# Pacing the last row gathers by their own landings and no longer by TensorE's progress

## The chip, the cores and the metric

The kernel runs on one core of a Trainium2 chip, and the time is the device time of one execution in microseconds (us). The kernel before takes 754.92 us, the median of three runs that lie between 752.6 and 755.72 us.

## The reference

The kernel computes one transformer block over 2048 tokens of 512 numbers: a cross-attention, and then a feed-forward part in which each token goes through two of eight experts and through one shared expert, which is kept here as two halves. Only the end of it matters for the change:

```python
wmat = (jax.nn.one_hot(topk_i, N_EXPERTS) * topk_w[..., None]).sum(axis=1)
e = jnp.einsum('ntf,nhf->nth', jax.nn.silu(g) * u, down_w)
routed = jnp.einsum('nth,tn->th', e, wmat)
shared = jax.nn.silu(sg) * su @ sh_down_w.T
return (routed + shared).reshape(B, S, H)
```

So every row of the output is the residual, plus the shared expert's result, plus two rows of expert results with two weights.

## The kernel before

Tokens are handled in 16 tiles of 128. The feed-forward part is a row of 68 units, numbered by `w`. A unit is one gate-and-up product (`gate_up`, 24 matmuls of 128x352, lines 1521 to 1525), a nonlinear step on ScalarE and VectorE, and one down product (`down`, 9 matmuls of 128x512, line 1538). Units 0 to 15 are the shared expert's two halves over the first eight tiles, units 16 to 51 are 36 slots of routed tokens (their results go to `slot_y` in DRAM), and units 52 to 67 are the shared halves over the last eight tiles. `C0` is 52, the number of the first late unit; `EARLY` is 8.

TensorE's order in the late units is: gate-and-up of `w`, down of `w-2`, gate-and-up of `w+1`, down of `w-1`, and so on. Between the two products of a unit lie, in this order: ScalarE's SiLU (line 1142), VectorE's product (line 2040), ScalarE's square (line 1147), VectorE's scale (2045), and the two fp16 parts of the hidden tile (ScalarE 1152, VectorE 2053). Then SyncE issues a DMA transpose of that tile into `hT` (`h_rows`, line 644). TensorE's down product waits for its landing (`hT_ld`), and so does the SiLU of the unit two later, because it overwrites the same hidden tile. Two `hT` tiles are used in turn.

GpSimd issues the gathers. For each of the 16 token tiles (numbered by `q`) two indirect DMAs of 128 rows of 2 KB, 256 KB together, read the tile's two expert results from `slot_y` (line 952) into `gather_1[q]` and `gather_2[q]`, each tile with buffers of its own. Ahead of the first one GpSimd waits until the last slot result has landed in DRAM (`y_st`). A semaphore `gat_ld[q % 4]` counts 32 for each tile. VectorE combines the gathered rows with the residual and the shared result in its late units (`early_out` for the first eight tiles, lines 2451 and 2455; `late_out` and `late_gathered` for the others, lines 2477, 2482, 2491, 2495), and each of these waits for `gat_ld`. GpSimd has nothing to do after the gathers.

All other late transfers are on SyncE's queue, in program order: in two units one activation tile (`load_late`), two residual tiles (`load_res`), two output tiles (`store_out`), 256 KB each, and the two transposes. `u_ready` counts the units whose up product is done on TensorE.

Of the kernel before, what the change touches and what calls it, by code (L numbers as in the profile page):

```python
# [84 lines left out]
def build(nc, x, ctxT, wqT, wkvT, wfcT, bfc, gwT, wgu, wdn, out):  # L85
# [17 lines left out]
    with ExitStack() as ctx:  # L103
# [3 lines left out]
        def sem(name):  # L107
            return ctx.enter_context(nc.semaphore(name))
# [287 lines left out]
        g_ready, u_ready, sil_done = sem("g_ready"), sem("u_ready"), sem("sil_done")  # L396
# [11 lines left out]
        B0, C0 = PA, PA + PB  # L408
# [375 lines left out]
        def _(pool):  # L784
# [160 lines left out]
                pool.wait_ge(y_st[s], FREE + 16 * ((SLOTS + 1 - s) // 2))  # L945
            for q in range(2 * EARLY):
                t = q // 2 + q % 2 * EARLY
                pool.wait_ge(u_ready, C0 + 3 + 2 * q // 3)
                if q >= 4:
                    pool.wait_ge(gat_ld[q % 4], q // 4 * 32)  # L950
                for to, idx in ((gather_1[q], p1_i), (gather_2[q], p2_i)):
                    nc.gpsimd.indirect_dma_start(  # L952
                        out=to, out_offset=None, in_=slot_y,
                        in_offset=bass.IndirectOffsetOnAxis(ap=idx[:, t:t + 1], axis=0)).then_inc(gat_ld[q % 4], 16)
# [1670 lines left out]
```

## Time and profile before

| | us |
|---|---|
| median of three runs | 754.92 |
| lowest, highest | 752.6, 755.72 |
| the profiled execution's own time | 754.92 |
| its span, first to last instruction | 753.1 |
| TensorE busy in the span | 732.2 |
| VectorE busy | 561.1 |
| ScalarE busy | 419.0 |
| GpSimd busy | 272.1 |
| mean share of the DMA engines, bytes per time | 223 GB/s over the span |

The span is what the profiler saw between the first and the last instruction; 1.8 us of the execution lie outside it. TensorE ran at its full granted clock of 2.4 GHz in all of it (mean 0.998 of full speed). A busy time is the time an engine was working, whatever waited for it; to find what sets the end, one has to ask which engine has no idle time in a stretch, and that is what the rows below are for.

### The profile page before, as it was taken

The numbers are of one execution on the slowest core, as the hardware profiler recorded it, in microseconds if no ns is written. First come the engines' busy times: TensorE is split into PE (matmuls) and PEld (weight loads), VectorE is DVE, ScalarE is ACT, GpSimd is POOL, SyncE is SP. The second block draws the span as 40 slices with busy tenths as digits, with TensorE's granted clock in tenths as the row PEclk, the third lists the DMA queues.
The fourth block names the chain that finished last, engine by engine and source line by source line (L and its number), as shares of the span: only waits on it lengthen the run. The fifth ranks groups of instructions, "written<-read, shape, count | busy, mean of one in ns | idle before, by whom it ended". The sixth has DMA issues, their size and how long they took to land.

```text
span 753.1 us, 16125 instructions
## 1 busy us (share of the span) xinstructions
PE 732.2 (97%) x5325; PEld 398.9 (53%) x5326; DVE 561.1 (75%) x1191; ACT 419.0 (56%) x845; POOL 272.1 (36%) x221
## 2 busy tenths in 40 slices
PE   6998999999999999999999999999999999999998
PEld 3554533434444334656665566555555556655554
DVE  4777689999999967788589998655555555546776
ACT  3667468888888884777543454343433334223222
POOL 3264006999997311664400401212111121016540
PEclk9999999999999999999999999999999999999999
DMA  9898946755755798997578664977767779549993
GB/s 328 332 409 282 252 147 187 221 168 176 220 150 151 249 344 301 345 386 281 190 204 259 153 155 123 197 175 181 184 168 184 173 180 213 127 124 283 329 308 92
DMA packets 155100, 168.17 MB, mean 223 GB/s; under 512 B 97952, under 2 KB 111776, under 8 KB 154528
## 3 DMA queue, kind: packets, MB, share of 16 engines
q1 hardware_dynamic: 143724, 126.20, 57.6%
q0 software_dynamic: 10720, 40.12, 17.0%
q10 hardware_dynamic: 596, 1.07, 0.4%
q8 instruction: 36, 0.59, 0.4%
q14 instruction: 24, 0.20, 0.1%
HBM read 104.09 MB, written 41.42 MB: 193 GB/s over the span
## 4 chain that ended last, share of the span: by engine, by line
PE 53%; DVE 23%; DMA 8%; issue 6%; POOL 4%; ACT 3%; SPq 2%; DVEq 0%; POOLq 0%; ACTq 0%
PE psum L1521 21%; DVE sb_rows L1786 12%; PE psum L1538 11%; PE psum L1523 4%; PE psum L1448 4%; PE psum L1257 4%; POOL sb_weights L952 4%; DMA sb_weights<-k_parts 2%; DMA sb_weights<-in_wdn 2%; PE psum L1540 2%; PE psum L1233 1%; DVE sb_rows L1915 1%; PE psum L1281 1%; DMA x_dram<-sb_rows 1%; DMA sb_rows<-xb_dram 1%
## 5 line engine op out<-in xcount | busy, mean ns | idle before, releaser
L1521 PE MATMUL psum<-sb_weights,sb_rows 128*128 128x352 f16 (+1 forms) x1344 | 209.7, 313 | 0.0
L1521 PEld LDWEIGHTS psum<-sb_weights,sb_rows 128*128 128x128 f16 x1344 | 131.2, 98 | 76.1 <-issue 1.2
L1786 DVE TENSOR_REDUCE sb_rows<-psum 128x4 f32<-128x1024 f32 x128 | 150.0, 1214 | 4.6 <-PE psum L1281 4.5
L1073 ACT ACTIVATE sb_weights<-psum 128x512 f32<-128x512 f32 x256 | 139.4, 595 | 22.8 <-PE psum L1353 19.7
L1538 PE MATMUL psum<-sb_weights,sb_hT 128*128 128x512 f16 (+1 forms) x522 | 122.2, 379 | 0.0
L1147 ACT ACTIVATE psum<-psum 128x352 f32<-128x352 f32 x68 | 30.5, 448 | 124.9 <-DVE psum L2040 112.3
L933 POOL DMA_INDIRECT sb_rows<-xn_rows,sb_slot_tok x36 | 34.6, 960 | 176.7 <-DVE sb_rows L2418 134.8
L1353 PE MATMUL psum<-sb_weights 50*128 50x512 f16 x256 | 86.6, 387 | 1.7 <-ACT sb_weights L1073 0.9
L1367 PE MATMUL psum<-sb_weights 128*32 128x256 f32 x1024 | 82.6, 394 | 0.3
L1538 PEld LDWEIGHTS psum<-sb_weights,sb_hT 128*128 128x128 f16 x522 | 50.9, 98 | 54.0 <-issue 0.6
L1281 PE MATMUL psum<-sb_weights 48*128 48x256 f16 x512 | 70.7, 274 | 1.6 <-DMA sb_weights<-k_parts 0.9
L1448 PE MATMUL psum<-sb_weights 128*128 128x512 f32 x128 | 58.3, 598 | 0.5 <-ACT sb_weights L1079 0.4
L2053 DVE SCALAR_TENSOR_TENSOR sb_h<-psum,sb_h_scale_i,sb_h 128x352 f16<-128x352 f32 x68 | 39.7, 583 | 22.7 <-ACT sb_h L1152 19.5
L952 POOL DMA_INDIRECT sb_weights<-slot_y,sb_p_i x32 | 32.5, 1015 | 64.4 <-DMA slot_y<-sb_rows 41.9
L2040 DVE SCALAR_TENSOR_TENSOR psum<-psum,sb_inv_now,sb_h 128x352 f32<-128x352 f32 x36 | 21.3, 592 | 43.6 <-issue 31.0
L1353 PEld LDWEIGHTS psum<-sb_weights 50*128 50x128 f16 x256 | 23.4, 93 | 54.2 <-ACT sb_weights L1073 44.7
L1142 ACT ACTIVATE sb_h<-psum,sb_inv_now 128x352 f32<-128x352 f32 x36 | 20.0, 555 | 49.4 <-PE psum L1521 37.7
L1257 PE MATMUL psum<-sb_weights 128*128 128x512 f16 x192 | 44.9, 380 | 2.3 <-DVE sb_weights L1852 1.2
L1152 ACT ACTIVATE sb_h<-psum,sb_h_scale_i 128x352 f16<-128x352 f32 x68 | 37.7, 555 | 16.2 <-DVE sb_h_scale_i L2045 14.8
L838 POOL TENSOR_TENSOR sb_weights<-sb_weights,sb_w_scale_i 128x1408 f32<-128x1408 f32 x15 | 38.0, 2533 | 23.6 <-ACT sb_weights L1119 22.8
L848 POOL TENSOR_TENSOR sb_weights<-sb_weights 128x1408 f16<-128x1408 f32 x15 | 43.0, 2864 | 1.2
L1142 ACT ACTIVATE sb_h<-psum,sb_w_inv_i 128x352 f32<-128x352 f32 x32 | 17.8, 556 | 33.1 <-PE psum L1521 22.7
(307 smaller groups left out, 1172.8 us busy)
## 6 DMA issues: line engine op xcount, KB each, us to landing
sb_weights<-in_wgu SPq DMA_DIRECT2D x20, 704.0 KB, 7.1
sb_weights<-in_wgu POOLq DMA_DIRECT2D x20, 704.0 KB, 6.8
sb_weights<-in_wdn SPq DMA_DIRECT2D x17, 768.0 KB, 6.3
slot_y<-sb_rows SPq DMA_DIRECT2D x36, 256.0 KB, 2.4
sb_weights<-q_parts SPq DMA_DIRECT2D x96, 64.0 KB, 3.0
x_dram<-sb_rows SPq DMA_DIRECT2D x24, 256.0 KB, 4.6
q_parts<-sb_weights SPq DMA_DIRECT2D x16, 256.0 KB, 4.1
sb_rows<-in_x POOLq DMA_DIRECT2D x16, 256.0 KB, 5.8
```

Source lines behind the costliest of these rows:

```text
L848: nc.gpsimd.tensor_tensor(low, stage, high, ALU.subtract).then_inc(gu_cut, 1)
L952: nc.gpsimd.indirect_dma_start(out=to, out_offset=None, in_=slot_y, in_offset=bass.IndirectOffsetOnAxis(ap=idx[:, t:t + 1], axis=0)).then_ ...
L1073: nc.scalar.activation(probs[G % 2][:, kt, pair * 512:(pair + 1) * 512], bank[4 + f % 2], ACT.Exp, scale=exp_by[n]).then_inc(exp_done, 1)
L1257: mm = nc.tensor.matmul(bank[Q_BANKS[n][m]], wq16[:, wp, k, m * P:(m + 1) * P], xnT[n % 2][:, xp, k, :], start=(k == 0 and i == 0), stop=( ...
L1281: mm = nc.tensor.matmul(bank[banks[qt] + side][:, h * SEQ:(h + 1) * SEQ], q_st[s][lo:hi, g, h, b * SEQ + qt * P:b * SEQ + (qt + 1) * P], k ...
L1353: nc.tensor.matmul(bank[4 + side].rearrange("p (h t) -> p h t", h=HH), k_st[s][lo:hi, g, b * SEQ + kt * P:b * SEQ + (kt + 1) * P], q_st[s] ...
L1367: mm = nc.tensor.matmul(bank[6][VW * c:VW * (c + 1), 0:SEQ], v_now, probs[G % 2][:, kt, c * SEQ:(c + 1) * SEQ], start=(kt == 0), stop=(kt ...
L1448: mm = nc.tensor.matmul(bank[2 + s][:], oT[s][:, k, :], wfc_sb[:, k, :], start=(k == 0), stop=(k == KD - 1))
L1521: mm = nc.tensor.matmul(to[:, 0:F], x_T[:, at:at + P], gu(wp, k, which), start=first, stop=last)
L1538: mm = nc.tensor.matmul(bank[Y_BANKS[par]][:], hT[par][:, hp, j, :], dn(wp, j), start=first, stop=last)
L1786: nc.vector.tensor_reduce(to[:, :, j // UB, :, j % UB, qt], psum[:, banks[qt] * 512:(banks[qt] + 2) * 512] .rearrange("p (a h k) -> p a h ...
L2053: nc.vector.scalar_tensor_tensor(h16[par][:, 1, 0:F], bank[GU_BANKS[par][1]][:, 0:F], h_scale[:, par:par + 1], h16[par][:, 0, 0:F], ALU.mu ...
```

## The change

The list of waits ahead of each tile's two gathers is made anew. Before, every tile waited until TensorE's up product of a unit fixed by `q` was done, and from `q` = 4 on also until the gathers of tile `q-4` had landed. After, tiles 1 to 3 wait for an up product, and tiles 4 to 15 only for the landing of tile `q-4`; tile 0 has no wait of its own.

```diff
@@ -945,9 +945,10 @@
                 pool.wait_ge(y_st[s], FREE + 16 * ((SLOTS + 1 - s) // 2))
             for q in range(2 * EARLY):
                 t = q // 2 + q % 2 * EARLY
-                pool.wait_ge(u_ready, C0 + 3 + 2 * q // 3)
                 if q >= 4:
                     pool.wait_ge(gat_ld[q % 4], q // 4 * 32)
+                elif q > 0:
+                    pool.wait_ge(u_ready, C0 + 2 + q)
                 for to, idx in ((gather_1[q], p1_i), (gather_2[q], p2_i)):
                     nc.gpsimd.indirect_dma_start(
                         out=to, out_offset=None, in_=slot_y,
```

The number that `u_ready` had to reach was 55, 55, 56, 57 for tiles 0 to 3, then 57, 58, 59, 59, 60, 61, 61, 62, 63, 63, 64, 65. It is now 55, 56, 57 for tiles 1 to 3 and nothing for the others.

## Rows read from the trace of the kernel before

**Rows 1.** The page: busy time of each engine; granted clock in 40 slices.
```profile
PE 732.2 (97%) x5325; PEld 398.9 (53%) x5326; DVE 561.1 (75%) x1191; ACT 419.0 (56%) x845; POOL 272.1 (36%) x221
PEclk9999999999999999999999999999999999999999
```
**Rows 2.** Timeline of TensorE, from 715 us; a bracket would show idle time.
```profile
720.92 2.11 PE L1538 MATMUL psum<-sb_weights,sb_hT 128*128 128x512 f16 x9
...
726.45 2.11 PE L1538 MATMUL psum<-sb_weights,sb_hT 128*128 128x512 f16 x9
...
744.96 1.24 PE L1711 MATMUL psum<-sb_weights,sb_hT 128*128 128x512 f16 x5
746.74 0.51 PE L1703 MATMUL psum<-sb_tri,sb_h 128*128 128x128 f16 x6 [0.54 <-DVE sb_h L2053]
```
**Rows 3.** Timeline of GpSimd, the gathers: start, duration, idle before.
```profile
674.07 0.94 POOL L952 DMA_INDIRECT sb_weights<-slot_y,sb_p_i  x1 [41.86 <-DMA slot_y<-sb_rows]
675.32 0.95 POOL L952 DMA_INDIRECT sb_weights<-slot_y,sb_p_i  x1 [0.30 <-issue]
...
683.15 0.95 POOL L952 DMA_INDIRECT sb_weights<-slot_y,sb_p_i  x1 [1.36 <-PE psum L1521]
...
685.66 0.95 POOL L952 DMA_INDIRECT sb_weights<-slot_y,sb_p_i  x1 [0.30 <-issue]
...
689.36 0.95 POOL L952 DMA_INDIRECT sb_weights<-slot_y,sb_p_i  x1 [0.98 <-PE psum L1521]
...
728.13 0.94 POOL L952 DMA_INDIRECT sb_weights<-slot_y,sb_p_i  x1 [0.30 <-issue]
```
**Rows 4.** Line 952: what ended GpSimd's idle time before a gather (us, times).
```profile
  DMA slot_y<-sb_rows: 41.9, 1
  PE psum L1521: 15.8, 9
```
**Rows 5.** Chain of waits from 716 to 727 us: start, length, what.
```profile
719.60 5.33 DMA sb_weights<-slot_y,sb_p_i
724.93 0.03 issue
724.96 0.76 DVE sb_weights L2477
```
**Rows 6.** Timeline of VectorE: first use of gathers; the operation ahead of 724.96 us.
```profile
679.44 0.74 DVE L2451 SCALAR_TENSOR_TENSOR sb_zero_row<-sb_weights,sb_w,sb_zero_row 128x512 f32<-128x512 f32 x1
...
724.46 0.58 DVE L2053 SCALAR_TENSOR_TENSOR sb_h<-psum,sb_h_scale_i,sb_h 128x352 f16<-128x352 f32 x1 [0.42 <-ACT sb_h L1152]
```
**Rows 7.** Timeline of SyncE's queue: two issues of the transpose of the hidden tile.
```profile
719.55 1.21 SPq L644 DMA_TRANSPOSE sb_hT<-sb_h  x1
...
741.62 1.21 SPq L644 DMA_TRANSPOSE sb_hT<-sb_h  x1
```
**Rows 8.** Timeline of ScalarE: the SiLU that a transpose released.
```profile
726.00 0.56 ACT L1142 ACTIVATE sb_h<-psum,sb_w_inv_i 128x352 f32<-128x352 f32 x1 [1.58 <-DMA sb_hT<-sb_h]
```
**Rows 9.** DMA from 686 to 730 us: busy tenths in 40 slices; packets; two queues.
```profile
DMA  9999999989999989999899999999999999999989
...
DMA packets 11928, 14.49 MB, mean 329 GB/s; under 512 B 7184, under 2 KB 7184, under 8 KB 11927
...
q1 hardware_dynamic: 9985, 8.10, 66.7%
q0 software_dynamic: 1942, 6.38, 41.5%
```
**Rows 10.** Windows: busy us by engine, granted clock, DMA share, GB/s.
```profile
685.00:690.00 5.00, 5.00 (x31) 2.89 (x30) 3.56 (x7) 1.29 (x3) 3.41 (x4) 1.00 1.23 360
...
707.00:718.00 11.00, 11.00 (x68) 6.41 (x66) 8.62 (x17) 3.10 (x8) 5.92 (x6) 1.00 1.07 367
718.00:729.00 11.00, 11.00 (x68) 6.41 (x67) 7.75 (x18) 3.50 (x11) 5.65 (x7) 1.00 1.07 304
729.00:740.00 11.00, 11.00 (x67) 6.45 (x66) 8.69 (x17) 3.10 (x7) 0.08 (x1) 1.00 0.65 194
```

## The prediction

> **What bounds the kernel now.** I read the page first: TensorE is busy in 97% of the span and at its full granted clock in every slice [rows 1]. Then I read the timeline of each engine over the stretch in which the gathers run, because GpSimd's busy time on the page says nothing of who waits for it. On TensorE's timeline one unit's down product starts at 720.92 us and the next one's at 726.45, so a unit lasts 5.53 us, and the rows carry no bracket, which is to say no idle time. The first idle time on TensorE after the gathers start is 0.54 us at 746.74, and it waits there for VectorE, for the last hidden tile [rows 2]. So from 674 us to the end the span is a sum of TensorE's own matmuls, with 0.54 us beside them.
>
> The gathers are issued from 674.07 to 728.13 us [rows 3]. The last slot result's landing holds the first one (41.9 us of idle time, once), and TensorE's up products hold nine later ones, 15.8 us together [rows 4]. Does anyone wait for a gather? The chain of waits says so: a gather issued at 719.60 takes 5.33 us and releases VectorE at 724.93 [rows 5]. But VectorE was in its operation of 724.46, 0.58 us long, up to then, and started the next one at 724.96 with no bracket [rows 6]. The landing and the end of the operation fell together. Nobody lost time to it, and TensorE was busy beside it.
>
> **The change, part by part.** *Tiles 0 to 3.* Tile 0 loses a wait for 55 up products; the one that ended last there was the landing of the slot result, so it starts at 674.07 as before [rows 3, 4]. For tiles 1, 2 and 3 the old numbers were 55, 56, 57 and the new ones are C0 + 2 + q = 55, 56, 57: the same. Cost 0, and the first eight gathers stay where they are. One of the nine waits for TensorE, that at 683.15, is tile 3's and stays [rows 3].
>
> *Tiles 4 to 15.* The other waits go; what is left is the landing of the tile four back. GpSimd issues one gather each 1.25 us when nothing holds it (674.07, 675.32) [rows 3], so a tile each 2.5 us, and three tiles and one gather lie between a tile's second gather and the tile four on: 3 x 2.5 + 1.25 = 8.75 us. A gather landed after 5.33 us with the DMA busy [rows 5]; the first tile's second gather, issued at 675.32, was used at 679.44, so at most 4.1 us after [rows 3, 6]. Both are under 8.75, so the wait that is left will mostly be open, and the change does what it says: from 685.66 on, 24 gathers in a row, the last issued at 685.66 + 23 x 1.25 = 714.4 us where it was 728.13, or 13.7 us earlier. On GpSimd nothing is queued behind, and no instruction is added; the wait instructions removed are GpSimd's. Gain on the path: nothing, as long as VectorE finds its rows in time, which it did. What idle time could be given back on TensorE is the 0.54 us at 746.74, and that is no gather's. So the gain is between 0 and 0.5 us; I take 0.
>
> *What the gathers now collide with.* The price can only come through the DMA engines. SyncE's queue carries the transposes of the hidden tile, and TensorE's down product waits for each. The one issued at 719.55 landed at 726.00, when the SiLU that it held was released (6.45 us), and TensorE started that unit's down product at 726.45 [rows 2, 7, 8]. That was 0.45 us to spare. With no gather about, the one issued at 741.62 had landed by 744.96, when its down product starts without idle time: at most 3.34 us [rows 2, 7]. So gathers and bulk transfers can cost a transpose 3 us, and there is room for 6.45 + 0.45 = 6.9 us.
>
> How full are the DMA engines? From 686 to 730 us every one of 40 slices shows 8 tenths or more; SyncE's queue (q1) takes 66.7% and the gathers (q0) 41.5%, together 108% [rows 9]. A share over 100% means that packets overlap, so I size it twice. By shares: 6.38 MB in gathers of 0.262 MB are 24 gathers, and 41.5% of 44 us is 18.3 us, or 0.76 us each. After, 24 gathers fall in 30 us: 24 x 0.76 / 30 = 61%, and with q1's 66.7% the sum is 128%, where the most that five us show is 1.23 and eleven us 1.07 [rows 10]. By bytes: q1 moves 8.10 MB / 44 us = 184 GB/s, the gathers after 6.3 MB / 30 us = 210 GB/s, together 394, against 367 in the best window of 11 us [rows 9, 10]. That is short by 7%, which over 30 us is 2.2 us of DMA work that doesn't fit.
>
> Who pays these 2.2 us? The gathers have 8.75 - 5.33 = 3.4 us before their own wait closes, and nobody needs them early. SyncE's queue has about half a microsecond to spare in the tightest unit. Bounds: below, 0 (the gathers give way, or the transposes that fall into slack of several us absorb it); above, 6 us (the first rival). I take the middle of the bytes' sum: 1.1 us of idle time on TensorE, in one to three down products between 690 and 720 us. From about 716 us on the gathers are gone and q1 is nearly alone, as from 729 on now (share 0.65) [rows 10]; the transpose of 719.55 then lands sooner than 6.45 us, which gives nothing back, because TensorE was not waiting for it.
>
> **Sum.** The profiled execution took 754.92 us, which is also the median; its span is 753.1, and 1.8 us lie outside. 754.9 - 0 + 1.1 = 756.0 us. The likeliest case's own range is 754.0 to 758.5.
>
> **The rivals.** *First, slower: turn by turn.* If each DMA engine shares itself half and half between the two queues whenever both have work, SyncE's queue gets 50% where it needs 66.7%. The 24 gathers hold 18.3 us of DMA work, so both queues contend for 36.6 us; in that time SyncE's queue does 18.3 us of work and needs 0.667 x 36.6 = 24.4. It falls 6.1 us behind, a slip that TensorE must wait for: 754.9 + 6.1 = 761.0. It decides from the point where a transpose takes over 6.9 us unit after unit; then the SiLU two units later is held as well [rows 8] and the loop feeds itself. For it: the 6.45 us at 719.55. Against it: q1 took 66.7% beside 41.5%, so it was not held to half, and GpSimd's own wait closes at 8.75 us.
>
> The Trainium skill, "DMA: Bandwidth & Descriptors", section "Queues, rings and completion order", says that each DMA engine goes round among the queues that have work and changes over a packet at a time. That is a rule that speaks against this change; by it the time would be nearer 761 than 756. The trace before agrees only so far that transposes are late when gathers are about, and doesn't show the turns.
>
> *Second, no effect: the gathers are hidden either way.* The transfers of SyncE's queue keep their pace, the shortfall falls on the gathers alone, and TensorE has no new idle time: 754.9 us. For it: windows with 1.23 and 367 GB/s without a gap on TensorE [rows 10]. Against it: the 0.45 us to spare.
>
> *Third, faster: the chain is right.* If the landing at 724.93 did hold VectorE, an earlier gather would start the following operations sooner; the profile gives 0.03 us there [rows 5], and TensorE can give back no more than 0.54 us [rows 2]: 754.4 us, still no change to be measured.
>
> **Chances.** What a measurement of this kernel can tell from no change is about 0.5%, or 3.8 us: under 751.1 or over 758.7. The forecast, 0.2 to 3.8 us slower, holds 0.50. The second rival holds 0.18, the third 0.06; both are within 0.5%. The first, over 758.7, holds 0.23. To a gain of over 0.5%, for which I can name no term, I leave 0.03. So faster 0.03, same 0.74, slower 0.23. The range reaches from 753.2 (the second and third with the scatter of the runs) to 760.0, into the first rival.
>
> **What would show it.** In the changed profile the last gather is issued near 714 us and line 952's idle time that TensorE ends falls from nine times to one, from 15.8 us to 1.4. If gathers reach 8.75 us, GpSimd's idle time is released by a DMA instead: the shortfall landed on the gathers. TensorE's first down products after 690 us show brackets that add up to 1 us (forecast), 0 (second) or 6 (first), and ScalarE's line 1142 waits for the transpose more often than once. The share after 720 us falls toward 0.65. The prediction is wrong if brackets on TensorE exceed 3.8 us, if the first eight gathers move, or if VectorE shows a wait for a gather at all.

## The result, and the profile after

The changed kernel takes 779.57 us (median of four runs, 776.47 to 780.23) where the kernel before takes 754.53 us (four runs, 752.6 to 755.72). The ratio is 1.0318 with a 95% interval of 1.0291 to 1.0346: 25 us slower, and 19.6 us over the upper end of my range.

The profiled execution took 776.41 us, among the fastest of the changed kernel, and 21.5 us more than the profiled one before. What the profiles explain is these 21.5 us; the other 3.5 us between the medians are in no profile.

The page of the changed kernel, to compare with [rows 1]: the engines do the same work, and the granted clock falls in two of the last four slices.

```profile
PE 737.8 (95%) x5325; PEld 399.1 (52%) x5326; DVE 562.1 (73%) x1191; ACT 418.6 (54%) x845; POOL 271.2 (35%) x221
PEclk9999999999999999999999999999999999996799
```

GpSimd's timeline of the changed kernel, to compare with [rows 3]. It did what I had forecast: the first eight gathers stayed, and the other 24 followed, most of them 1.25 us apart (three take 1.3 to 1.5 us and not 0.95, so the mean is 1.30), the last at 714.95. One gather is 128 rows of 2 KB, so 256 KB; a tile's two are 512 KB together, and not 256 as the description of the kernel has it.

```profile
682.44 0.94 POOL L953 DMA_INDIRECT sb_weights<-slot_y,sb_p_i  x1 [2.10 <-PE psum L1522]
683.69 0.95 POOL L953 DMA_INDIRECT sb_weights<-slot_y,sb_p_i  x1 [0.30 <-issue]
...
714.95 0.95 POOL L953 DMA_INDIRECT sb_weights<-slot_y,sb_p_i  x1 [0.30 <-issue]
```

TensorE's timeline of the changed kernel, where [rows 2] have no bracket before 746.74. In the brackets stands the idle time before and what ended it.

```profile
694.34 1.78 PE L1522 MATMUL psum<-sb_weights,sb_rows 128*128 128x352 f16 x9
696.92 0.61 PE L1522 MATMUL psum<-sb_weights,sb_rows 128*128 128x352 f16 x3 [0.80 <-issue]
699.05 0.61 PE L1522 MATMUL psum<-sb_weights,sb_rows 128*128 128x352 f16 x3 [1.52 <-issue]
...
711.06 0.59 PE L1539 MATMUL psum<-sb_weights,sb_hT 128*128 128x512 f16 x1 [2.38 <-issue]
713.16 0.59 PE L1539 MATMUL psum<-sb_weights,sb_hT 128*128 128x512 f16 x1 [1.51 <-issue]
...
720.72 5.73 PE L1522 MATMUL psum<-sb_weights,sb_rows 128*128 128x352 f16 x24
726.29 2.10 PE L1539 MATMUL psum<-sb_weights,sb_hT 128*128 128x512 f16 x9
728.23 3.74 PE L1522 MATMUL psum<-sb_weights,sb_rows 128*128 128x352 f16 x24
```

The same two units in the kernel before, from its timeline of TensorE:

```profile
695.25 3.74 PE L1521 MATMUL psum<-sb_weights,sb_rows 128*128 128x352 f16 x24
...
706.30 3.74 PE L1521 MATMUL psum<-sb_weights,sb_rows 128*128 128x352 f16 x24
```

One gate-and-up product starts at 694.34 us. After its first nine matmuls the others come in threes, twos and ones; I call this the crawl. The idle time ends by "issue", which is to say that no semaphore and no transfer was waited for. Single matmuls start 0.7, 1.4 or 2.1 us after each other, once 2.8, where a product at full pace has one each 0.15 us. At about 719.5 us, 3.6 us after GpSimd's last gather was issued, it is over.

From 694.34 to 728.23 us TensorE does two units in 33.89 us, where the kernel before takes 706.30 - 695.25 = 11.05: 22.8 us lost. The two spans differ by less, 774.3 - 753.1 = 21.2. The changed execution was 0.9 us ahead when the crawl began, and from 728.23 on it takes 46.1 us where the one before takes 46.8 from 706.30 on, mostly because the 0.54 us at 746.74 [rows 2] have gone: VectorE had caught up. So the crawl is the whole loss of this execution. The brackets are 14.6 us of it, the rest is matmuls at half clock and in small groups. (At 720.72 a full product takes 5.73 us instead of 3.74: the clock granted after the crawl is still 1.2 GHz and costs 2 us of it.)

Windows of the changed kernel (busy us by engine, granted clock, DMA share, GB/s). In the crawl TensorE is soon at half clock (it falls at 700.9 us), GpSimd alone keeps its pace, and the DMA engines are less busy than ahead of it.

```profile
685.00:694.50 9.50, 9.50 (x58) 5.43 (x57) 6.37 (x13) 1.67 (x4) 7.46 (x7) 1.00 1.09 311
700.00:712.00 12.00, 4.37 (x10) 0.81 (x10) 2.91 (x6) 1.11 (x3) 9.26 (x10) 0.54 0.74 216
```

### The profile page after: what moved, and what is told of

Read it like the earlier page. It is cut to its first block, busy times and chain, and to the rows that moved or that the text cites. A ratio compares the mean times of both kernels' runs of the same rounds, so it can differ in the third digit from the quotient of the medians.

```text
span 774.3 us, 16113 instructions
## 1 busy us (share of the span) xinstructions
PE 737.8 (95%) x5325; PEld 399.1 (52%) x5326; DVE 562.1 (73%) x1191; ACT 418.6 (54%) x845; POOL 271.2 (35%) x221
## 4 chain that ended last, share of the span: by engine, by line
PE 63%; DVE 19%; DMA 9%; issue 5%; SPq 2%; ACT 2%; DVEq 0%; ACTq 0%
PE psum L1522 28%; PE psum L1539 15%; DVE sb_rows L1787 11%; PE psum L1524 4%; PE psum L1258 4%; PE psum L1449 3%; DMA sb_weights<-k_parts 3%; PE psum L1541 2%; DMA sb_weights<-in_wdn 2%; DMA sb_rows<-xb_dram 2%; PE psum L1234 2%; DMA sb_weights<-in_x 1%; DVE sb_rows L1916 1%; PE psum L1282 1%; PE psum L1239 1%
## 5 line engine op out<-in xcount | busy, mean ns | idle before, releaser
L1522 PE MATMUL psum<-sb_weights,sb_rows 128*128 128x352 f16 (+1 forms) x1344 | 214.6, 315 | 7.7 <-issue 7.6
L1539 PE MATMUL psum<-sb_weights,sb_hT 128*128 128x512 f16 (+1 forms) x522 | 125.0, 383 | 7.2 <-issue 7.0
L2054 DVE SCALAR_TENSOR_TENSOR sb_h<-psum,sb_h_scale_i,sb_h 128x352 f16<-128x352 f32 x68 | 39.6, 582 | 22.7 <-ACT sb_h L1153 21.2
L838 POOL TENSOR_TENSOR sb_weights<-sb_weights,sb_w_scale_i 128x1408 f32<-128x1408 f32 x15 | 38.0, 2533 | 23.6 <-ACT sb_weights L1120 22.8
L1143 ACT ACTIVATE sb_h<-psum,sb_w_inv_i 128x352 f32<-128x352 f32 x32 | 17.8, 555 | 52.2 <-PE psum L1522 28.8
```

The lines of the kernel that those rows point to most:

```text
L838: nc.gpsimd.tensor_tensor(stage, stage, scale.broadcast_to([P, HALF]), ALU.mult).then_inc(gu_scaled, 1)
L1522: mm = nc.tensor.matmul(to[:, 0:F], x_T[:, at:at + P], gu(wp, k, which), start=first, stop=last)
L1539: mm = nc.tensor.matmul(bank[Y_BANKS[par]][:], hT[par][:, hp, j, :], dn(wp, j), start=first, stop=last)
L2054: nc.vector.scalar_tensor_tensor(h16[par][:, 1, 0:F], bank[GU_BANKS[par][1]][:, 0:F], h_scale[:, par:par + 1], h16[par][:, 0, 0:F], ALU.mu ...
```

## Experiments

Each is one kernel, in most cases a single run with its profile, beside the kernel before (752.9 to 754.1 us). All but one edit the changed kernel; the one that moves the row is given as an edit of the kernel before. The kernels with a quarter of the bytes, a quarter of the rows or plain copies leave out a part of the work and give a wrong result.

**Spacing by landings.**

```diff
                 if q >= 4:
                     pool.wait_ge(gat_ld[q % 4], q // 4 * 32)
+                    pool.wait_ge(gat_ld[(q - 1) % 4], (q - 1) // 4 * 32 + 32)
```

The second kernel has q - 2 in place of q - 1.

> From tile 4 on a tile's two gathers wait for the landing of the tile just before, instead of the tile four back; no wait for TensorE. Theory 1 (an unbroken stream of gathers starves TensorE's own issue of matmuls, and the removed waits broke the stream): the stream has a pause of some 3 to 4 us after each tile, so TensorE shows no brackets and the time is that of the kernel before, 753 to 757 us. Theory 2 (what counts is that gathers run while TensorE goes through certain units, wherever the pauses are): the last gather still comes early and the time stays above 765 us.

It took 783.27 us. That is over the second theory's 765, but by a way that neither theory names. TensorE has no crawl, but two long idle stretches of 8.87 and 13.31 us that VectorE ends, and VectorE waited for gathers. GpSimd's and VectorE's waits in this kernel (us, times, longest):

```profile
POOL sb_weights L954 <- DMA sb_weights<-slot_y,sb_p_i: 51.1, 12, 5.2
DVE sb_weights L2453 <- DMA sb_weights<-slot_y,sb_p_i: 27.0, 5, 10.5
```

A tile now takes about 6.4 us and the last gather is issued at 762.69: too late, and the time goes another way. So the run has little to say of the crawl, but it shows the other edge: the gathers have room to be late, and not as much as 35 us.

> From tile 4 on a tile waits for the landing of the tile two back. Two tiles take 5 us to issue and a gather lands some 4 to 5 us after its issue, so the pauses are short, 1 to 2 us per tile, or none. Theory 1: between the kernel before and the changed one, 756 to 775 us, with fewer brackets on TensorE. If pauses of any length do, 754 to 757. Theory 2: above 765 us.

It took 757.88 us, between the two as expected: no crawl, but TensorE's down products waited 1.77 and 0.43 us for transposes within the loop and 1.32 us behind it, ScalarE waited six times for one (13.5 us), and VectorE twice for gathers (3.7 us).

**A quarter of the bytes, then a quarter of the rows.**

```diff
+                quarter = slot_y.rearrange("r (c d) -> (r c) d", c=4)
...
-                        out=to, out_offset=None, in_=slot_y,
+                        out=to if q < 4 else to[:, 0:D // 4], out_offset=None, in_=slot_y if q < 4 else quarter,
```

> The changed kernel with the gathers of tiles 4 to 15 cut to a quarter of each row (512 B instead of 2 KB; three quarters of the columns, and the right rows, are left out). GpSimd issues the same 24 indirect DMAs back to back, each 1.25 us, with a quarter of the bytes. If the bytes on the DMA engines starve TensorE: 753 to 757 us, no brackets. If GpSimd's issuing does it (the descriptors it writes, the semaphores): still above 770 us.

It took 775.91 us with the same crawl (first bracket at 695.23). From 700 to 712 us the DMA engines were all but idle and TensorE did 9 matmuls:

```profile
700.00:712.00 12.00, 3.76 (x9) 0.86 (x9) 1.62 (x5) 1.11 (x3) 8.95 (x11) 0.50 0.18 49
```

```diff
+                    if q >= 4:
+                        to, idx = to[0:32, :], idx[0:32]
```

> The changed kernel with the gathers of tiles 4 to 15 cut to 32 of 128 rows (the other 96 rows are left out), so the same number of indirect DMAs with a quarter of the descriptors. If each instruction keeps its length and the crawl stays (above 770 us): what starves TensorE is GpSimd's unbroken row of such instructions, not what it hands to the DMA engines. If the crawl goes (753 to 757 us): it is the descriptors.

It took 781.0 us. GpSimd's instruction is a little shorter (0.87 us), so the gathers come each 1.17 us, and the crawl came sooner (693.89) and was slower, 6 matmuls in the same window:

```profile
700.00:712.00 12.00, 2.86 (x6) 0.52 (x5) 0.97 (x2) 0.00 (x0) 8.81 (x11) 0.50 0.33 73
```

The crawl stays with a quarter of the bytes and with a quarter of the rows, at DMA shares of 0.18 and 0.33. That rules out the DMA engines' load as the cause.

**The row of gathers moved to a later place.** Tiles 0 to 8 wait as before the change, the others are free. Against the kernel before:

```diff
-                pool.wait_ge(u_ready, C0 + 3 + 2 * q // 3)
+                if q < 8:
+                    pool.wait_ge(u_ready, C0 + 3 + 2 * q // 3)
+                if q == 8:
+                    pool.wait_ge(u_ready, C0 + 3 + 2 * q // 3)
                 if q >= 4:
                     pool.wait_ge(gat_ld[q % 4], q // 4 * 32)
```

> Tiles 0 to 8 wait as in the kernel before; tiles 9 to 15 only for the landing of the tile four back. So 16 gathers run without a break from about 700 to 720 us, when TensorE is in the second pass of its loop over the late tiles; in the changed kernel it stalled in the first pass, 11 us after the stream began. Theory 1 (density, wherever): TensorE crawls again from some 10 us into the stream until its end, 760 to 770 us. Theory 3 (TensorE's first pass through that code is what is starved): no brackets, 753 to 757 us.

It took 765.96 us. TensorE's timeline in this kernel:

```profile
710.43 2.10 PE L1541 MATMUL psum<-sb_weights,sb_hT 128*128 128x512 f16 x9
712.38 0.61 PE L1524 MATMUL psum<-sb_weights,sb_rows 128*128 128x352 f16 x3
713.59 0.31 PE L1524 MATMUL psum<-sb_weights,sb_rows 128*128 128x352 f16 x1 [0.60 <-issue]
```

The row begins at 700.68, the first bracket comes 12.9 us later, in other units and in a later pass of the loop. In the changed kernel it is 696.92 - 682.44 = 14.5 us. The crawl follows the row and not the place.

**TensorE's loop written out.** `with pe.Fori(1, (TILES - EARLY) // 2) as i:` became `for i in range(1, (TILES - EARLY) // 2):`.

> The changed kernel with TensorE's loop over the late tiles written out, so that its instructions are read once each and none twice. If the crawl belongs to the loop: 753 to 757 us. If TensorE's supply of instructions as such is starved: the crawl comes as before or sooner, 770 us or more.

It took 775.79 us, with the first bracket at 698.95 us. The hardware loop is not needed for it.

**Three real breaks.** The old wait for TensorE on tiles 7, 10 and 13 only.

```diff
+                if q in (7, 10, 13):
+                    pool.wait_ge(u_ready, C0 + 3 + 2 * q // 3)
```

> The changed kernel with the old wait for TensorE put back for tiles 7, 10 and 13 only. In three kernels TensorE began to crawl 12 to 13 us after the start of an unbroken row of gathers. If the length of the unbroken row decides: rows of 3 tiles are 7.5 us, so no brackets of 0.6 us or more on TensorE and 753 to 757 us. If the mean rate of the gathers decides, or gathers far ahead of their use: 765 us or more.

It took 754.18 us beside 753.51, without a bracket on TensorE. GpSimd's timeline shows the row cut into a piece of eight gathers and three of six, by breaks of 0.94, 3.85 and 3.62 us. The second of them:

```profile
700.01 0.94 POOL L955 DMA_INDIRECT sb_weights<-slot_y,sb_p_i  x1 [0.30 <-issue]
704.79 0.94 POOL L955 DMA_INDIRECT sb_weights<-slot_y,sb_p_i  x1 [3.85 <-PE psum L1524]
```

The breaks also make the row slower, 1.61 us a gather on the mean, so this run by itself doesn't tell whether the breaks or the mean spacing let TensorE on.

> The kernel with the old wait for TensorE on tiles 7, 10 and 13 only, timed in five rounds beside the kernel before. All theories that stand: TensorE has no idle time to give back but the half microsecond before its last transposes, so the ratio to the kernel before is 0.998 to 1.002.

The same kernel in twelve runs: median 756.03 us, ratio 1.0033 (1.0019 to 1.0047). That is over my upper line by 0.1%. Its profile is that of the slowest of the twelve (760.06 us). There TensorE's down products wait twice for a transpose:

```profile
712.53 2.11 PE L1541 MATMUL psum<-sb_weights,sb_hT 128*128 128x512 f16 x9 [1.56 <-DMA sb_hT<-sb_h]
719.28 2.12 PE L1541 MATMUL psum<-sb_weights,sb_hT 128*128 128x512 f16 x9 [1.06 <-DMA sb_hT<-sb_h]
```

**Pauses on GpSimd that wait for nobody.** A memset of 128x296 with its own semaphore behind each gather (or two of them).

```diff
                         in_offset=bass.IndirectOffsetOnAxis(ap=idx[:, t:t + 1], axis=0)).then_inc(gat_ld[q % 4], 16)
+                    for _ in range(1 if q >= 4 else 0):
+                        pauses += 1
+                        nc.gpsimd.memset(tile_cmp[:], 0.0).then_inc(pstep, 1)
+                        pool.wait_ge(pstep, 5 + pauses)
```

The second kernel has `2 if q >= 4 else 0`.

> The changed kernel with a short memset on GpSimd (128x296, waited for) behind each gather of tiles 4 to 15; no wait for TensorE or for landings beyond the changed kernel's. Gathers then come each 1.7 us instead of 1.25. If a short pause after each gather is enough to let TensorE on: 753 to 757 us. If only a row without a real break counts (GpSimd busy all the time): as the changed kernel, 770 us or more.

It took 754.21 us, no crawl, at a spacing of 1.6 us and with GpSimd idle for 0.3 us between its instructions, once for 0.9.

> The same with two memsets behind each gather, so one gather each 2.1 us and the last one issued near 735 us, later than in the kernel before. If pauses free TensorE: no crawl, but VectorE may wait for gathers at the end, 754 to 762 us. If GpSimd's being busy in any way starves TensorE: worse than the changed kernel.

It took 760.19 us: no crawl, but VectorE waited 4.8 us for a gather, and a transpose came 2.2 us late for TensorE. So a GpSimd that is kept busy otherwise does no harm here; its indirect DMAs in a tight row do.

The same memset only behind each tile, only behind each second tile (5, 7, 9, 11, 13), only behind tiles 6, 9 and 12:

> One short memset (waited for) behind each tile's two gathers, from tile 4 on; the mean rate is one gather each 1.4 us, nearer to the changed kernel's 1.25 than to the 1.6 with a memset behind each gather. If a pause resets TensorE's trouble: 753 to 757 us without crawl. If it is the rate of issue, somewhere between 1.6 (no crawl) and 1.25 (crawl): a crawl that begins later than 12.6 us into the row, 757 to 772 us.

> The memset behind tiles 5, 7, 9, 11 and 13: mean spacing of the gathers about 1.34 us, between the 1.30 (crawl) and the 1.43 us (none) of the kernels with one pause in three tiles and in each tile. If mean spacing decides and the limit is not far below 1.43: a crawl, begun later than 12.6 us into the row, 758 to 774 us. If a pause after four gathers resets: 753 to 757 us.

> The memset only behind tiles 6, 9 and 12, so three pauses of about 0.5 us in a row of 26 gathers at otherwise full rate; no unbroken row is longer than 10 us. If any pause resets the count: no crawl, 753 to 757 us. If TensorE falls behind by the mean rate, or needs a real break of 2 us and more as with the three waits for TensorE: a crawl as in the changed kernel, 768 us or more.

They took 752.63, 773.59 and 776.12 us. I had put the mean spacings too low in all three, because some gathers take 1.3 to 1.5 us and not 0.95. Measured from the first gather of the row to the last, over the number of steps ("crawl after" is the time from the row's first gather to TensorE's first row with a bracket):

```
kernel                      first, last gather    steps   spacing   crawl after    us (one run; changed: median)
quarter of the rows         683.17  712.98         25     1.19      10.7 us        781.0
waits on ScalarE (below)    680.67  711.99         25     1.25      10.0 us        778.8
row moved                   700.68  719.86         15     1.28      12.9 us        766.0
loop written out            683.08  715.29         25     1.29      15.9 us        775.8
quarter of the bytes        682.08  714.44         25     1.29      13.2 us        775.9
changed kernel              682.44  714.95         25     1.30      14.5 us        779.6
memset behind 3 tiles       682.53  716.06         25     1.34      13.3 us        776.1
memset behind 5 tiles       681.79  715.86         25     1.36      15.2 us        773.6
memset behind each tile     680.56  718.19         25     1.51      none           752.6
three real breaks           682.22  722.53         25     1.61      none           754.2
memset behind each gather   682.50  723.45         25     1.64      none           754.2
```

A memset behind a tile widens one step by 0.3 us, and three or five of them reset nothing. Over the whole row the kernels sort by their mean spacing, and it turns between 1.36 and 1.5 us. That the mean alone decides is not shown. The kernel with three real breaks issued its first 14 gathers in 17.8 us, 1.37 us apart, with one break of 0.94 us among them, and had no bracket; the one with a memset behind three tiles crawled after 13.3 us, with its gathers 1.39 us apart up to there. A break in which GpSimd stands idle may count for more than its length, or the limit lies close to 1.37; no run here separates the two.

> The kernel with one memset behind each tile's two gathers, timed in five rounds. TensorE has no idle time left to give back but half a microsecond: ratio to the kernel before 0.997 to 1.003. Late transposes (2.9 us of ScalarE's waits in its one look) may cost a little: not over 1.005.

In twelve runs the memset behind each tile gives 757.02 us (754.12 to 762.75), ratio 1.0051 (1.0027 to 1.0075), at the very end of what I had allowed. At 1.49 us its profile has no crawl, but ScalarE is held back five times by "remote", 13.2 us in all, two of them (4.0 us each) like this:

```profile
693.64 0.55 ACT L1148 ACTIVATE sb_h<-psum,sb_w_inv_i 128x352 f32<-128x352 f32 x1 [3.96 <-remote]
```

Three of its runs are 7 to 9 us slower than the fastest. What makes them so isn't shown; their granted clock is 0.996 to 0.998 on the mean, where the changed kernel's crawl left 0.98. The single run at 752.63 had promised a gain that the timing doesn't bear out. No version that I tried beats the kernel before.

**Plain copies in place of the gathers.**

```diff
+                if q >= 4:
+                    for to in (gather_1[q], gather_2[q]):
+                        nc.gpsimd.dma_start(to, slot_y_tiles[q]).then_inc(gat_ld[q % 4], 16)
+                else:
...
```

> The changed kernel with the 24 gathers of tiles 4 to 15 replaced by plain copies of the same size that GpSimd issues back to back (one slot tile each; they bring the wrong rows). Same bytes, same queue, no index. If it is the indirect form that starves TensorE: 753 to 757 us. If any row of transfers issued by GpSimd does: 765 us or more.

It took 775.86 us, and by another way. A copy costs GpSimd 0.55 us, so eight of them are soon outstanding, GpSimd then waits for landings, and the transposes queue up behind the copies. TensorE waits for them in whole products and has no crawl:

```profile
706.19 3.66 PE L1543 MATMUL psum<-sb_weights,sb_hT 128*128 128x512 f16 x9 [2.84 <-DMA sb_hT<-sb_h]
...
716.30 3.72 PE L1543 MATMUL psum<-sb_weights,sb_hT 128*128 128x512 f16 x9 [2.87 <-DMA sb_hT<-sb_h]
...
729.89 3.76 PE L1543 MATMUL psum<-sb_weights,sb_hT 128*128 128x512 f16 x9 [6.28 <-DMA sb_hT<-sb_h]
```

TensorE waits four times so, 15.3 us in all, and from 690 to 715 us the two queues take 57.2% (q0, the copies) and 52.1% (q1): near the even split of my first rival, and dearer than its 6.1 us. The run answers for no more than these copies: since GpSimd's own waits break its row, the run can't tell whether plain copies in a tight row would make TensorE crawl.

**Many instructions on ScalarE.** Behind each late unit, `for _ in range(50): act.wait_ge(consts, 2)`, on a semaphore long set.

> The changed kernel with 50 more waits on ScalarE at the end of each late unit, each on a semaphore that is long set, so that ScalarE has a dense row of instructions too (some 17 ns each, about 1 to 3 us in a unit; it has 3 us of idle time in each). If any engine with many instructions starves while the gathers are issued: ScalarE's waits come 0.7 us apart in the crawl, as TensorE's matmuls do. If TensorE alone starves: they keep their pace. Time 774 to 785 us either way.

It took 778.8 us. The starts of ScalarE's added waits that the trace has (us), in the row of gathers from 680.67 to 711.99 and after it (in brackets, how many within 0.1 us):

```
682.77 to 684.19: 16 of them
684.92 (2)  685.63  686.34 (2)  687.76 (3)  688.50  691.31 (2)  692.05  692.75  694.15  694.86  695.58  696.97 ...
719.74 to 721.56: 25 of them
```

ScalarE starves in the same way: from 3.5 us after the start of the row on its instructions come 0.7 us or 1.4 us apart, and after the row they run 25 in 1.9 us again. It starves even in the first six gathers, which start at 671.11 and which every kernel here has: from 676.32 to 679.91 its waits come with steps of 0.6, 1.4, 0.7 and 0.9 us. TensorE's crawl came sooner in this kernel, 10.0 us after the start of the row. The added waits read and write no tile, so a contention for operands is not needed to slow them. Its ordinary work was held up too, by "issue":

```profile
689.25 0.55 ACT L1143 ACTIVATE sb_h<-psum,sb_w_inv_i 128x352 f32<-128x352 f32 x1 [5.92 <-issue]
```

So TensorE isn't singled out: it is the engine that goes through most instructions (a weight load and a matmul each 0.15 us).

## Why the prediction was wrong

*What held.* TensorE without idle time set the tail; the first eight gathers stayed; the wait that was left was never closed (line 953 is released by a DMA only for the first gather); 24 gathers followed at 1.25 to 1.30 us, the last at 714.95 where I had 714.4; nobody waited for a gather, and nothing was won. Of the third rival no more is seen than that the 0.54 us went, behind the crawl. My own sign of being wrong came true: TensorE's brackets add up to 14.6 us, where I had allowed 3.8.

*The step that failed* is the sentence "The price can only come through the DMA engines". I had costed GpSimd's issuing as free for others, since nothing is queued behind it on its own engine. In the changed kernel the crawl took 22.8 us, more than the 21.2 by which the spans differ, while the DMA share fell to 0.74 and SyncE's queue carried little (8.4% from 694 to 720 us). With a quarter of the bytes (share 0.18) it stayed; with the same gathers each 1.64 us it was gone. That GpSimd's tight row of indirect DMAs causes it is shown by these pairs. What exactly it takes from the other engines is not: the trace shows only that instructions without any wait come 0.7 us apart, that the two engines with a dense row of them both suffer, and that TensorE's crawl begins 10 to 16 us into the row. I read this as a supply of instructions that the issuing holds up, and engines that first use up what they have; argued, not shown. A rival that no run tests is that semaphore updates and the ends of instructions are held up, and engines stop when too many are outstanding. The kernel before has a sign of it: the last matmul of a gate product starts at 680.33 and lasts 0.31 us, but its semaphore event is recorded at 682.77, and that of the up product behind it, started at 682.12, at 682.90.

The Trainium skill, "Runtime: NRT & Kernel Launch", section "Instruction fetch mechanics", says that an engine's instruction memory is refilled in 16 KiB blocks by a DMA queue of its own. This case's page agrees with the size: queue q8 of kind "instruction" carries 35 packets and 0.57 MB in the changed kernel, 16 KB each. A starved refill would be the obvious story, and the trace doesn't bear it out. From 694 to 720 us no packet of an instruction queue is recorded, as this view of the changed kernel's DMA shows. That by itself proves little, because the kernel before has none from 689 to 740 us either, at full pace. But the kernel with the loop written out needs new instructions all the time: it has a block on q8 at 722.94, 744.36 and 766.06 us, where the kernel before has its last two at 681.10 and 749.25. Ahead of 722.94 its last block is at 682.12, and its crawl lies between the two: the first gap at 698.95, the last at 720.16. So the crawl ended without a refill. I take q8 to be TensorE's queue, from these numbers alone.

```profile
q0 software_dynamic: 1590, 5.20, 63.9%
q1 hardware_dynamic: 446, 0.79, 8.4%
```

*The term I did price,* late transposes, is real, but its size is not confirmed. In the kernel with three breaks my sum's 1.1 us stand against 0 in the single run (754.18) and 1.56 + 1.06 us of waits on TensorE in the profile at 760.06, the slowest of twelve; the ratio of the twelve, 1.0033, is 2.5 us. In the changed kernel the term could not come up, because TensorE crawled first. My first rival (761 us by turns) was nearer in time, for a cause that wasn't there; the copies show what late transposes look like, with a median of 16.3 us from a transpose's issue to its landing (690 to 715 us).

*Could the trace before have told?* It had a trace of it. These are ScalarE's SiLUs in the kernel before that waited for "remote", 6.9 us together:

```profile
682.88 0.56 ACT L1142 ACTIVATE sb_h<-psum,sb_w_inv_i 128x352 f32<-128x352 f32 x1 [3.97 <-remote]
...
721.81 0.56 ACT L1142 ACTIVATE sb_h<-psum,sb_w_inv_i 128x352 f32<-128x352 f32 x1 [2.91 <-remote]
```

They waited on TensorE's gate products, which by TensorE's own rows were done 2.2 to 2.6 us earlier; both come at the end of a stretch of four to six gathers at 1.25 us. I read [rows 8] for the one wait that a transpose ended and passed over these two. And the waits for TensorE had a side I didn't see: when TensorE falls behind, `u_ready` comes late and GpSimd stops, so by the code the old pacing could not run far ahead of a slowed TensorE. The landing wait gives no such feedback: in the changed kernel it is never closed, all through the crawl.

## What to carry to other kernels

Treat an engine's issuing of DMAs as work that can cost others time, whatever the DMA engines' load: here a row of GpSimd indirect DMAs 1.36 us or less apart on the mean, kept up for 10 us or more, slowed TensorE to a crawl. Before you remove a wait as redundant, ask what rate it limits and whether it ties the fast engine to the slow one; a wait for the consumer's progress is feedback, a wait for a landing is not. In a trace, a lot of idle time ended by "issue" or "remote" on an engine that has its data is a finding in itself.

## What the runs showed of the hardware

- While GpSimd issued indirect DMAs each 1.19 to 1.36 us on the mean, TensorE fell after 10.0 to 15.9 us to one matmul per 0.7, 1.4 or 2.1 us. It recovered 3.6 us after the last was issued (719.5 against 715.9 us) in the changed kernel. In the kernels at 1.5 us and more there was no crawl. It stayed with a quarter of the bytes (775.9 us) and a quarter of the rows (781.0 us).
- ScalarE with a dense row of waits that were all satisfied fell to the same steps of 0.7 us, 3.5 us into the row.
- A plain copy of 256 KB costs GpSimd 0.55 us to issue, an indirect one 0.95 with 0.30 behind it. With up to eight copies outstanding a transpose on SyncE's queue took 16.3 us to land (median of three), where it took at most 3.34 us with no gather about and 6.45 us beside one.
- The granted clock fell from 2.4 to 1.2 GHz at 700.9 us, with TensorE in the crawl, and rose again at 724.7, when TensorE had been without a gap since 719.5. The first full product behind the crawl took 5.73 us instead of 3.74.
- In the kernel before, beside a stretch of gathers 1.25 us apart, two semaphore events of TensorE's gate products were recorded 2.1 and 2.5 us after the matmul's end.
